# A post-norm transformer layer with top-31 attention: one product less in the threshold's matmul group, two banks for transposed scores, one bank for everything else

## What is computed

```python
# x: 16 batches of 512 rows of 256; 16 heads of 16
Q, K, V = (x @ W.T + b).reshape(B, L, H, D).transpose(0, 2, 1, 3)
scores = einsum('bhqd,bhkd->bhqk', Q, K) / sqrt(D)
thresh = top_k(scores, 31)[0][..., -1:]
attn = softmax(where(scores < thresh, -inf, scores))
context = einsum('bhqk,bhkd->bhqd', attn, V)...reshape(B, L, 256)
x = layernorm(x + context @ Wo.T + bo)
gate, up = x @ wg.T, x @ wu.T            # int32 weights / 127, 768 hidden
x = layernorm(x + (silu(gate) * up) @ wd.T)
```

## Time and profile before

| | |
|---|---|
| median of 3 runs | 3084.57 us |
| lowest, highest | 3081.59, 3086.80 us |
| the profiled execution's own time | 3082.59 us |
| its span in the profile | 3080.8 us |
| mean granted TensorE clock | 0.954 of full speed |
| busy, share of the span | PE 89%, DVE 81%, ACT 81%, POOL 78% |
| instructions | 81076 |

### The profile page before, as it was taken

The page is one execution under the profiler, slowest core; times in us unless marked ns, Lnnn a source line. Parts: engine busy times, 40 slices in busy tenths (PEclk is TensorE's granted clock), DMA queues, the critical chain, the costliest instruction groups (busy, mean ns, idle before and its releaser), DMA issues.

```text
span 3080.8 us, 81076 instructions
## 1 busy us (share of the span) xinstructions
PE 2733.1 (89%) x21030; PEld 1498.6 (49%) x21375; DVE 2502.0 (81%) x12298; ACT 2496.6 (81%) x5894; POOL 2401.5 (78%) x1677
## 2 busy tenths in 40 slices
PE   5988989899998998889989998988989998998986
PEld 2444545455454454544545454444545545454554
DVE  4888888888888878888888888878888888888851
ACT  4888888888889877788888888878878887898852
POOL 1888887788788877788788787877878787788881
PEclk7899999999999999999999999999999999999987
DMA  2201011110111101011010111102111010111000
GB/s 85 48 20 44 22 50 29 28 44 24 38 27 40 38 22 42 19 43 36 25 45 25 37 29 36 39 20 47 25 35 37 25 44 26 36 30 32 20 16 7
DMA packets 91143, 102.64 MB, mean 33 GB/s; under 512 B 34513, under 2 KB 52946, under 8 KB 90578
## 3 DMA queue, kind: packets, MB, share of 16 engines
q1 hardware_dynamic: 88544, 93.73, 12.7%
q10 hardware_dynamic: 2034, 2.76, 0.3%
HBM read 20.86 MB, written 8.39 MB: 9 GB/s over the span
## 4 chain that ended last, share of the span: by engine, by line
PE 51%; ACT 19%; issue 14%; DVE 12%; SPq 1%; POOL 1%; ACTq 1%; DVEq 1%; DMA 0%; POOLq 0%
ACT above L479 8%; PE bench L681 6%; PE Y_ps L617 6%; PE ST_ps L628 6%; PE bench L687 6%; PE ST_ps L631 6%; PE ctxT_ps L645 5%; ACT junk L469 5%; DVE cand L877 5%; PE bench L558 4%; PE Y_ps L615 4%; ACT PT L487 3%; PE Y_ps L614 3%; PE bench L674 2%; PE bench L589 2%
## 5 line engine op out<-in xcount | busy, mean ns | idle before, releaser
L1109 POOL TENSOR_SCALAR mask<-S,thr,mb 128x512 bf16<-128x512 f32 x1024 | 2114.0, 2077 | 42.9 <-POOL mb L1103 34.6
L877 DVE MAX8 cand<-Y_ps 128x8 f32<-128x128 f32 x4096 | 1075.5, 283 | 6.7 <-issue 6.7
L870 DVE TENSOR_SCALAR_CACHE_REDUCE S<-S_ps,na 128x512 f32<-128x512 f32 x1024 | 758.1, 740 | 298.7 <-PE S_ps L604 240.7
L469 ACT ACTIVATE junk<-S,at_zero,slope 128x512 bf16<-128x512 f32 x1024 | 824.8, 805 | 96.5 <-DVE S L870 96.5
L479 ACT ACTIVATE above<-S,s,steep 128x512 bf16<-128x512 f32 x1024 | 825.1, 806 | 0.6
L487 ACT ACTIVATE PT<-ST_ps 128x512 f32<-128x512 f32 x1024 | 596.9, 583 | 224.2 <-PE ST_ps L631 222.9
L628 PE MATMUL ST_ps<-QS,KS 64*128 64x512 f32 x1024 | 457.3, 447 | 122.2 <-ACT PT L487 117.0
L604 PE MATMUL S_ps<-KS,QS 64*128 64x512 f32 x1024 | 523.5, 512 | 4.2 <-DVE S L870 2.8
L617 PE MATMUL Y_ps<-KS,QS 64*128 64x512 f32 x1024 | 523.1, 511 | 1.0 <-issue 0.7
L615 PE MATMUL Y_ps<-above,nbig 128*128 128x512 bf16 x1020 | 399.0, 391 | 74.9 <-DVE cand L877 49.6
L631 PE MATMUL ST_ps<-nbig,mask 128*128 128x128 bf16 x4096 | 417.9, 226 | 0.0
(11 more groups left out here) (125 smaller groups left out, 3681.5 us busy)
## 6 DMA issues: line engine op xcount, KB each, us to landing
QS<-Qhi SPq DMA_DIRECT2D x512, 32.0 KB, 2.0
KS<-Khi SPq DMA_DIRECT2D x512, 32.0 KB, 2.0
KS<-Klo SPq DMA_DIRECT2D x512, 32.0 KB, 2.0
QS<-Qlo SPq DMA_DIRECT2D x512, 32.0 KB, 2.0
xTs<-in_xT SPq DMA_DIRECT2D x17, 512.0 KB, 3.8
xs<-in_x SPq DMA_DIRECT2D x16, 512.0 KB, 3.9
out<-xs SPq DMA_DIRECT2D x16, 512.0 KB, 2.9
hT<-in_wgT ACTq DMA_DIRECT2D x1, 768.0 KB
```

Of the source, the lines that this page charges most:

```text
L469: nc.scalar.activation(junk[:, :], S[:, score_place(j)[0], :], ACT.Tanh, bias=at_zero[:, :], scale=slope[:, hb, col:col + 1], accum_out=s0 ...
L870: nc.vector.tensor_scalar(S[:, at, :], S_ps[n % 2][:, :], na[:, hb, col:col + 1], None, ALU.add, op1=ALU.max, accum_out=rmax[:, n % RING:n ...
L877: mx = nc.vector.max(cand[:, j % CANDS, i, :], Y_ps[j % 2][:, i * BW:(i + 1) * BW])
L1109: nc.gpsimd.tensor_scalar(mask[:, h % MASKS, t, :], S[:, score_place(j)[0], :], thr[:, r:r + 1], mb[:, r:r + 1], ALU.is_lt, op1=ALU.add).t ...
```

## The change

1. `ST_ps` becomes two banks, used in turn by tile. PE's wait moves one tile back (`exp_done, T - TURNED - 1`).
2. The bench becomes one bank with one `ready` and one `taken` semaphore. Each use waits for the use before it.
3. The slots are set anew so that every slot has one use: q from 11 to 10, keys 13 to 14, gram 14 to 17, quad 15 to 19, sums 17 to 21 and 56 to 55, the turned context from (27, 28) to (28, 29), gate products in 42, 44, 46, 49, 51, 53, up products in 43, 45, 47, 50, 52, 54.
4. `th` has two halves, used in turn. ACT's tanh waits for POOL's product before last, and the copy of up for the last one.
5. DVE takes the output projection, the second half of x1 and the down product before its `evacuate` of the slot, where it did so after it. The row statistics stay behind it.
6. ACT's sign is written as unsigned bytes into the upper byte of each bf16 of `above`, whose lower bytes are set to zero once at the start. A byte of 1 reads as the bf16 number 2^-125, and -1 is to become 0. It is multiplied with -2^127 (`nbyte`), which gives -4 above the threshold and nothing below. The constant pass (L614) and `ones_b` go.
7. To keep -4 far below every score, the weights and the bias of k are multiplied by 2^-38 at the start, BIG is 4, and the exponential's scale takes the factor back.
8. The flags and the column of ones are bf16 where they were float32.
9. `brow` and its three parts, used once after the first batch, lie in `th` and `ups`; ACT waits for their load before it begins the second batch.

```diff
-BIG = 2.0 ** 40
+SHIFT = 2.0 ** -38
+BIG = 4.0
+BYTE_BIG = 2.0 ** 127
...
-HALF_USES = {4: "v", 11: "q", 12: "k", 13: "keys", 14: "gram", 15: "quad", 17: "sums",
-             26: "v", 33: "q", 34: "k", 35: "keys", 36: "gram", 37: "quad", 56: "sums"}
+HALF_USES = {4: "v", 10: "q", 12: "k", 14: "keys", 17: "gram", 19: "quad", 21: "sums",
+             26: "v", 33: "q", 34: "k", 35: "keys", 36: "gram", 37: "quad", 55: "sums"}
-CTX_T, OUT_PROJ, X1_T = (27, 28), (30, 31), (38, 39)
-FFN_SLOTS = {43: 0, 45: 1, 47: 2, 50: 3, 52: 4, 54: 5}
+CTX_T, OUT_PROJ, X1_T = (28, 29), (30, 31), (38, 39)
+GATE_SLOTS = {42: 0, 44: 1, 46: 2, 49: 3, 51: 4, 53: 5}
+UP_SLOTS = {43: 0, 45: 1, 47: 2, 50: 3, 52: 4, 54: 5}
...
-        onesc = sb("onesc", [P, 1])
+        onesc = sb("onesc", [P, 1], BF16)
-        th = sb("th", [P, L])
+        th = sb("th", [P, 2, L])
-        flag = sb("flag", [P, 2, PAIR + 1])
+        flag = sb("flag", [P, 2, PAIR + 1], BF16)
-        ST_ps = ps("ST_ps", [P, L])
+        ST_ps = [ps(f"ST_ps{i}", [P, L]) for i in range(2)]
-        bench = [ps(f"bench{i}", [P, L]) for i in range(2)]
+        bench = ps("bench", [P, L])
...
-                nc.scalar.activation(above[:, j % 4, :], S[:, score_place(j)[0], :], ACT.Sign, bias=s0[:, j % 8:j % 8 + 1],
+                nc.scalar.activation(above[:, j % 4, :].bitcast(U8).rearrange("p (l y) -> p l y", y=2)[:, :, 1], S[:, score_place(j)[0], :], ACT.Sign, bias=s0[:, j % 8:j % 8 + 1],
...
-                nc.scalar.activation(PT[:, j % 4, :], ST_ps[:, :], ACT.Exp, scale=SCALE).then_inc(exp_done, 1)
+                nc.scalar.activation(PT[:, j % 4, :], ST_ps[j % 2][:, :], ACT.Exp, scale=SCALE / SHIFT).then_inc(exp_done, 1)
...
                         if what == "gate":
-                            act.wait_ge(ready[k], use + 1)
+                            act.wait_ge(ready, use + 1)
+                            if part > 1:
+                                act.wait_ge(h_done, (b - 1) * NF + part - 1)
+                            nc.scalar.activation(th[:, part % 2, :], bench[:, :], ACT.Tanh, scale=0.5 * DEQ).then_inc(th_done, 1)
+                        if what == "up":
+                            act.wait_ge(ready, use + 1)
                             if part:
                                 act.wait_ge(h_done, (b - 1) * NF + part)
-                            nc.scalar.activation(th[:, :], bench[k][:, :], ACT.Tanh, scale=0.5 * DEQ).then_inc(th_done, 1)
-                        if what == "up":
-                            act.wait_ge(ready[k], use + 1)
-                            nc.scalar.activation(ups[:, :], bench[k][:, :], ACT.Copy, scale=0.5 * DEQ * DEQ).then_inc(taken[k], 1)
+                            nc.scalar.activation(ups[:, :], bench[:, :], ACT.Copy, scale=0.5 * DEQ * DEQ).then_inc(taken, 1)
...
-                nc.tensor.matmul(Y[:, :], nbig[:, :], ones_b[:, :], start=True, stop=False)
-                nc.tensor.matmul(Y[:, :], nbig[:, :], above[:, j % 4, :], start=False, stop=False)
+                nc.tensor.matmul(Y[:, :], nbyte[:, :], above[:, j % 4, :], start=True, stop=False)
...
-                if not (first and n == TURNED):
-                    pe.wait_ge(exp_done, T - TURNED)
+                ST = ST_ps[j % 2]
+                if not (first and n < TURNED + 2):
+                    pe.wait_ge(exp_done, T - TURNED - 1)
...
             def on_bench(b, n, first, rest):
                 for what, part in uses_of(n, first, rest):
-                    k, use = place(b, n, what, part, first, rest)
-                    pe.wait_ge(taken[k], use)
+                    use = place(b, n, what, part, first, rest)
+                    pe.wait_ge(taken, use)
...
-            nc.vector.memset(ones_b[:, :], 1.0)
+            nc.vector.memset(above[:, :, :], 0.0)
...
+            nc.vector.tensor_scalar(nbyte[:, :], ident[:, :], -BYTE_BIG, None, ALU.mult)
+            nc.vector.tensor_scalar(bqk[1][:, :], bqk[1][:, :], SHIFT, None, ALU.mult)
+            nc.vector.tensor_scalar(wqk[1][:, :, :], wqk[1][:, :, :], SHIFT, None, ALU.mult).then_inc(consts_done, 1)
```

More of the change, by code:

```diff
@@ L44 @@
 RANKS = 16
-TINY = 1.0e-30
+TINY = 1.0e-36
 COUNT0 = 1
@@ L128, with count @@
 TURN_OF, ACT_TURN_OF = 5, 7
[L130 to L138, removed]
+def count(first, rest, upto=(TILES, None)):
+    have = 0
     for n in range(TILES):
@@ L142, in counts @@
                 return have
-            have[BANKS[n, use]] += 1
+            have += 1
     return have
-PROLOGUE_COUNT = [len(PROLOGUE[0::2]), len(PROLOGUE[1::2])]
-FIRST_COUNT = counts(True, False)
-BATCH_COUNT = counts(False, False)
+FIRST_COUNT = count(True, False)
+BATCH_COUNT = count(False, False)
 def place(b, n, what, part, first, rest):
-    k = BANKS[n, (what, part)]
-    have = counts(first, rest, (n, (what, part)))[k]
+    have = count(first, rest, (n, (what, part)))
     if first:
[L157 to L162, removed]
+        return len(PROLOGUE) + have
+    return (b - 1) * BATCH_COUNT + (len(PROLOGUE) + FIRST_COUNT + have)
 def build(nc, xT, x, wqT, wkT, wvT, woT, bq, bk, bv, bo, wgT, wuT, wdT, ident_in, blocks_in, heads_in, ranks_in, out):
@@ L380, in steps @@
                     stack(h)
-                k, use = place(b, VALUES_AT[1], "v", 0, first, False)
-                wait_apart(sp, ready[k], use + 1)
+                use = place(b, VALUES_AT[1], "v", 0, first, False)
+                wait_apart(sp, ready, use + 1)
                 load_xT(b if last else b + 1)
@@ new lines, in slots @@
+                        if what == "out_proj":
+                            if part == 0:
+                                dve.wait_ge(x_loaded, b * 16)
+                            residual((2 * part, 2 * part + 1), use)
+                        if what == "x1_t":
+                            dve.wait_ge(x1T_copied, b * 2 - 1 + part)
+                            to = [x1T[j][:, :, part * 2 * P:(part + 1) * 2 * P].rearrange("p c (n t) -> p n c t", n=2)
+                                  for j in range(2)]
+                            nc.vector.tensor_tensor(to[1], bench[:, :].rearrange("p (n c t) -> p n c t", n=2, c=C),
+                                                    to[0].bitcast(F32), ALU.subtract).then_inc(taken, 1)
@@ L1031, in slots @@
+                        if what == "down":
+                            residual((part,), use)
                         if what == "turn":
-                            normalise((n - 1 - GROUP) // 16 % NG, b * NG + n // 16 - 1, (k, use))
+                            normalise((n - 1 - GROUP) // 16 % NG, b * NG + n // 16 - 1, use)
                     for part in range(3):
@@ L1139, in slots @@
                     for what, part in uses_of(n - 1, first, rest) if n else []:
-                        if what == "gate":
-                            k, use = place(b, n - 1, "gate", part, first, rest)
-                            pool.wait_ge(taken[k], use + 1)
                         if what == "up":
-                            k, use = place(b, n - 1, "up", part, first, rest)
-                            pool.wait_ge(taken[k], use + 1)
-                            nc.gpsimd.tensor_tensor(hT[:, part, :], th[:, :], ups[:, :], ALU.mult).then_inc(h_done, 1)
+                            use = place(b, n - 1, "up", part, first, rest)
+                            pool.wait_ge(taken, use + 1)
+                            nc.gpsimd.tensor_tensor(hT[:, part, :], th[:, part % 2, :], ups[:, :], ALU.mult).then_inc(h_done, 1)
                     if not rest and HALF_USES.get(n - 4) == "sums":
```

317 lines of the change are left out of this document (141 added, 176 removed).

## The result

The changed kernel takes 3113.36 us (median of 4 runs, 3109.12 to 3120.91) against 3085.69 us before: 1.0095 times as long, with a 95% interval of 1.0073 to 1.0117. It was forecast to be 3.3% faster and is 0.95% slower.

The account below looks back on a forecast made before the run. PE was taken as first bound, with three engines close behind. Batches -126, other slots -11, flags -3, preparation +2 and clock +35 summed to -103 us on 3082.6, giving 2980 us; own range 2940 to 3020, overall range 2850 to 3060.

Parts of the forecast that it names:

- G: Seventh of eight 8-tile stretches of a batch: 24.50 us, to become 23.1 (-1.4), then bound by POOL.
- D: Fourth of eight 8-tile stretches of a batch, PE-bound: 21.08 to 25.20 us class; forecast 22.5 us (-2.7).
- A: First stretch of a batch, tiles 1 to 8, bound by ACT: 19.70 us, forecast 19.2 (-0.5).
- the 0.9 us that I had left over: Per stretch, time beyond the busiest other engine's busy time, taken to remain when PE is no hindrance.
- H: Last stretch of a batch, tiles 57 to 64, with down products, PE-bound: 26.80 us, forecast 24.1 (-2.7).
- The single bench bank: Nothing in the sum; as rival, 20 slots a batch lose 0.3 us each, 90 us back, 3070 us; chance 0.13.
- The removed pass: Constant pass L614 in every slot: 0.22 us a slot saved, 1.76 us per 8-slot stretch where PE sets the pace.
- The second bank for transposed scores: PE's 226 us wait for exponentials, 1.8 us a stretch, would go; half counted, 0.9 us a stretch.
- The clock: Lighter PE stretches bring 10 us more half clock per batch, at 0.23 us each: 2.3 a batch, +35 us.
- C: Third of eight stretches of a batch, bound by DVE: 18.50 us, forecast 19.45 (+0.95); one extra half-clock fall expected here.
- E: Fifth of eight stretches of a batch, bound by ACT: 22.80 us, forecast 21.65 (-1.15).
- The better packing: Rival: stretches go halfway to their busiest other engine, 65 us less; about 2910, 2850 without clock term; chance 0.15.

Follow-up runs that it names:

- E6: The changed kernel with one bank for transposed scores instead of two, one bench bank kept: 3210.8 us, ratio 1.0393 to the kernel before.
- E3: The changed kernel with two bench banks in turn and one bank for transposed scores: 3068.6 us, ratio 0.9935 to the kernel before.
- E10: The changed kernel with two bench banks, one bank for transposed scores, and a zero-weight pass added in every slot: 3064.0 us, ratio 0.9921.
- E5: The changed kernel with two bench banks, one ST_ps, and a zero-weight pass in slots 0-12, 14-27 and 36-40: 3036.6 us, ratio 0.9825.
- E1: The changed kernel with a zero-weight pass, as long as the removed one, put back into every slot: 3105.2 us, ratio 1.0049.
- E12: The changed kernel, one bench bank throughout, with a zero-weight pass in slots 0-4, 8-10, 14-27, 38-42 and 55-57: 3079.5 us, ratio 0.9986.
- E7: The kernel before with byte writes, scaled keys and removed pass, plus a zero-weight pass in slots 0-12, 18-27 and 36-40: 3081.5 us, ratio 0.9984.
- E2: The kernel before with only the byte writes, scaled keys and removed pass; old slots and banks: 3124.2 us, ratio 1.0105.
- E9: The kernel before, nothing removed, with a zero-weight pass added in slots 0-4, 18-24, 36-39 and 55-57: 3063.9 us, ratio 0.9930.
- E4: The changed kernel with a second bench bank, taken from S_ps, in the last short pass alone: 3103.3 us, ratio 1.0041 to the kernel before.
- E8: The changed kernel, second bench bank in the last pass, zero-weight pass in slots 0-4, 8-10, 14-27, 38-42 and 55-57: 3049.3 us, ratio 0.9874.

## Why the prediction was wrong, step by step

- **What bounds the kernel** was read rightly in the main: PE first, three engines close behind. G and D came out at 22.6 and 23.0 us against 23.1 and 22.5 forecast, A at 17.2 against 19.2: the 0.9 us that I had left over was not there, and ACT was busy for less. The whole batch took 180.1 us where 171.2 was forecast, 5.8 of the 8.9 in H alone.
- **The single bench bank** is the step that failed most. In the sum it stood at nothing; in a rival, with 0.13 of the chance, at 90 us. E6 against E3 measured 141 us, as large as all that I had forecast to be gained. I had priced it by one pair, gate and its product on DVE, and assumed that PE's own work covers it. The sign that I had named for this came true: the weight loads of the gate and up products (L678) wait 0.58 us each for DVE's product (54.8 us, 95 times). The larger single waits are elsewhere, where a use in the next slot follows one that DVE takes late: the first down product behind the turned context (33.6 us, 14 times), and the q and k projections behind each other (L555, 45.3 us, 18 times). The four down products themselves do not hold one another up: in all they wait 4.3 us for DVE. In H the wait of 2.87 us is followed by half clock, which is not there in E3, and the two cost 5.5 us.
- **Head and last pass** were never looked at for what they are: stretches in which nothing lies beside the bench's chain. I gave them -11 us; the head is 5 us longer and the last pass 23.5 us. There each product waits in full for ACT and DVE, and PE, drawn apart by the waits, does its twelve products at half clock: 8 us of waits and 10.7 us of slower passes.
- **The removed pass** is the other step that failed. It was forecast at 1.76 us a stretch where PE sets the pace; by itself it gives 7.5 us a batch in my sum, or 112 us, and 77 us after the clock's 35. E3 against E10 measured a loss of 4 us with the clock it costs included, which is nothing within the intervals. With most of the clock held up, removing it from the heavy half of the slots brings 30 us (E10 against E5), 19 to 26 (E1 against E12), and 5 in the kernel before (E7). The 0.22 us of the earlier trace rows are not in doubt, but PE mostly arrives earlier at another wait, as the 311.8 us in E2 (226.0 before) suggest.
- **The second bank for transposed scores** was worth more than my sum gave it. The 0.9 us a stretch count there only where PE sets the pace: 1.8 us a batch on top of the removed pass (27 us in 15), 5 on its own (75 us). E6 measured 92 us against the changed kernel, with one bench bank in both.
- **The clock** had the right sign and the wrong size. I expected 10 us more at half clock a batch, 150 in all; it is 394 us more. Some 47 of these are in the last pass (clock 0.58 against 0.70) and 22 a batch in the rest, within the ends of that estimate (0 and 60) but twice its value. At my price the term is 91 us and not 35. The place was half right: C has its share, but H has more, E nearly as much and A none. The price of 0.23 us for each us is borne out: E9 shows 0.23 (22 us for 93), and E3 to E5, E4 to E8, E2 to E7 and the changed kernel to E12 show 0.16, 0.15, 0.11 and 0.12, all net of the time of the added passes, so the full price is higher. That the clock can fall without a long pause of PE holds for the earlier trace rows, where PE's idle pieces are 0.95 to 1.46 us; but in H half clock follows a wait for the bench, and in the last pass it stays through such waits, and these I had not counted.
- **The byte writes** cost nothing, as taken: 0.810 us for L473 against 0.806 before.

Three figures of the prediction do not follow from its own terms. The better packing with no term for the clock is 2910 - 35, some 2875, and 2850 is the whole way with that term. With two thirds of its price the bench rival gives 3040; the range's 3060 takes eight ninths. And with the clock's 35 us paid, 103 us of gain are lost at 0.34 us a slot and not at 0.45.

The rival that came true is the one of the bench bank: its 141 us are some 9 a batch, or 0.45 us a slot for 20 slots, and I gave it too little. That the clock and the bench would come together, and that waits for the bench would cost clock, I had in no case.

Put together by ratio, from E10 (two benches, one `ST_ps`, PE streaming as before, -24 us against the kernel before): the removed pass, the clock it costs included, +4 us to E3; the single bench +141 to E6; the second bank for transposed scores -92 to the changed kernel; in all +29, which is the result. The steps add up by construction; in another order each could have another size, and two benches with two banks for transposed scores, which would need a ninth PSUM bank, were not measured. So the new slots, the double `th`, DVE's new order and the bf16 flags (with the byte form, whose time E10 has put back, and the rewritten form) are worth 24 us together. They were not taken apart.

What stays open: how much of the bench's 110 us in the batches is waits and how much is the half clock that follows them (in H and in the last pass it is about half each), and why E4's batches are longer than those of the changed kernel.

## What to carry to other kernels

Taking away the second of two buffers is not free merely because most hand-overs fit beside other work. Look for the places where one use directly follows another that is read late, and for the head and the drain of the pipeline, where nothing lies beside them. A wait of the matmul engine can cost twice, once as a wait and once as the half clock after it. Before taking work from a matmul engine that is only half the bottleneck, look at its granted clock in the lightest stretches, and after it at the mean clock first of all; a pass of zero weights in just those slots is a cheap test, and here the cure. A removed piece of work gains only what the next wait on the same engine leaves over, so remove that wait first.

## What the hardware showed that I had not expected

- Dead matmuls make a kernel faster: 22 us for one 512-column pass of zero weights in 19 of 64 slots of the kernel before (E9), whose clock rose from 0.954 to 0.969.
- The clock answers steeply to a small change of load. One pass less in each slot took the time at half clock from 283 to 681 us (E2), and the same pass back in 28 of 64 slots to 345 us (E7).
- Products drawn apart by waits can stay at half clock for as long as they last: 38.9 us at a clock of 0.50 with PE busy for 24.89 of them (the changed kernel's last pass), where two banks brought the clock to full by the third product (E4).
- ACT writes single bytes two bytes apart at the rate of whole bf16 numbers: 810 ns against 806 for 512 elements.
